# Attention of three layers in units of 256 rows, on row and column tiles of TensorE

## What is computed

```python
xn = _layernorm(x)
s = attention_k(xn)            # k = 0 to 3
g = _silu(ffn_k(xn))
x = x + s * g
```

```python
# layer 0: 16 query heads of 64, one head of keys and values, 2 null keys,
#          l2-normed q and k; the first 64 keys are open to every query
# layer 1: 16 heads of 64, each with its own keys and values
scores = einsum('bhsa,bhta->bhst', q, k) * scale
pattern = softmax(where(causal, scores, -1e5), axis=-1)
z = einsum('bhst,bhta->bsha', pattern, v); out = einsum('bsha,had->bsd', z, Wo) + bo
# layer 3: 16 heads of 8, no output product
```

## Time and profile before

| | us |
|---|---|
| median of three runs | 5998.41 |
| lowest run | 5994.97 |
| profiled execution, its span | 5995.4 |
| attention of layer 0, first scores to end of loops | 82 to 644 |
| the same, layer 1 | 1024 to 1573 |
| the same, layer 3 | 5158 to 5720 |

### The profile page before, as it was taken

The page is one execution under the profiler, slowest core; times in us unless marked ns, Lnnn a source line. Parts: engine busy times, 40 slices in busy tenths (PEclk is TensorE's granted clock), DMA queues, the critical chain, the costliest instruction groups (busy, mean ns, idle before and its releaser), DMA issues. The chain is left out here.

```text
span 5995.4 us, 91995 instructions
## 1 busy us (share of the span) xinstructions
PE 4804.1 (80%) x27408; PEld 3412.1 (57%) x27408; DVE 3795.6 (63%) x8398; ACT 3211.5 (54%) x9294; POOL 1986.0 (33%) x1579
## 2 busy tenths in 40 slices
PE   6888897999864446888888888888888887688888
PEld 4667664666631104566666666666666665466666
DVE  5555223444558886777777777777777776455522
ACT  4444343555323335666666766666766665244433
POOL 3333100222204553444444444444444442122200
PEclk8888998999975558999999999999999999688899
DMA  0000000000000001000000000000000000000000
GB/s 16 1 2 2 33 0 19 2 2 2 13 3 0 0 0 47 1 0 21 0 0 21 0 0 21 0 0 21 0 0 0 0 0 1 16 1 0 0 28 7
DMA packets 26030, 41.55 MB, mean 7 GB/s; under 512 B 12208, under 2 KB 18376, under 8 KB 25160
## 3 DMA queue, kind: packets, MB, share of 16 engines
q1 hardware_dynamic: 25800, 38.86, 1.9%
HBM read 36.75 MB, written 2.10 MB: 6 GB/s over the span
## 5 line engine op out<-in xcount | busy, mean ns | idle before, releaser
L1380 PE MATMUL ps<-l2f_wqkv,l2f_xsT 128*128 (+3 forms) x1536 | 741.6, 606 | 96.5 <-DVE xnT L1575 90.5
L1312 POOL TENSOR_TENSOR l2f_rn<-l2f_ss,neghalf 128x16 f32<-128x16 f32 x192 | 564.7, 2941 | 436.2 <-DVE l2f_ss L1569 436.2
L1757 ACT ACTIVATE l2f_p<-ps,l2f_negmax 128x96 f32<-128x96 f32 x1536 | 501.7, 339 | 281.8 <-DVE l2f_negmax L1600 278.2
L1318 POOL TENSOR_TENSOR l2f_cosd<-xnT,l2f_rot 128x1024 f32<-128x1024 f32 x192 | 487.0, 2541 | 174.8 <-DVE xnT L1575 174.8
L1438 PE MATMUL ps<-l2f_pT,l2f_vw 96*128 96x128 f32 x3072 | 419.7, 280 | 39.2 <-DVE l2f_pT L1622 38.9
L1380 PEld LDWEIGHTS ps<-l2f_wqkv,l2f_xsT 128*128 128x128 f32 (+1 forms) x1536 | 243.4, 178 | 347.4 <-issue 197.2
L1772 ACT COPY l2f_oT<-ps 64x256 f32<-64x256 f32 x768 | 281.3, 366 | 268.1 <-PE ps L1438 256.4
L1438 PEld LDWEIGHTS ps<-l2f_pT,l2f_vw 96*128 96x128 f32 x3072 | 379.4, 194 | 59.4 <-issue 54.2
L1338 POOL TENSOR_TENSOR l2f_rstd<-l2f_mv,neghalf 128x1 f32<-128x1 f32 x96 | 52.8, 550 | 1045.9 <-DVE l2f_mv L1634 1045.9
L1411 PEld LDWEIGHTS ps<-l2f_kT,l2f_qz 128*128 128x128 f32 x3072 | 398.3, 194 | 1.5 <-issue 0.4
L1411 PE MATMUL ps<-l2f_kT,l2f_qz 128*128 128x96 f32 x3072 | 397.9, 273 | 0.0
(11 more groups left out here) (348 smaller groups left out, 12274.8 us busy)
## 6 DMA issues: line engine op xcount, KB each, us to landing
l2f_wqkv<-L_ffn_Wqkv_dram SPq DMA_DIRECT2D x18, 512.0 KB
l0f_w<-L_w_dram SPq DMA_DIRECT2D x2, 2304.0 KB
l3f_w<-L_w_dram SPq DMA_DIRECT2D x2, 2048.0 KB
l2f_wo<-L_ffn_Wo_dram SPq DMA_DIRECT2D x6, 512.0 KB
l2f_w<-L_ffn_W_dram SPq DMA_DIRECT2D x6, 341.0 KB
l2f_b<-L_ffn_b_dram SPq DMA_DIRECT2D x6, 341.0 KB
l1f_w<-L_w_dram SPq DMA_DIRECT2D x1, 1152.0 KB
k_turn<-l3a_kF SPq DMA_DIRECT2D x4, 256.0 KB, 2.0
```

The source lines that it names most:

```text
L1312: nc.gpsimd.tensor_tensor(rn[:, k], ss[:, k], g.neghalf[:, 0:HEADS], ALU.pow).then_inc(rn_ready, 1)
L1318: nc.gpsimd.tensor_tensor(cosd[:, k].rearrange("p (h d) -> p h d", d=DH), nrm[:, k].rearrange("p (h d) -> p h d", d=DH), rot[:, k, 0, t].u ...
L1380: ins = nc.tensor.matmul(g.ps[0:rows, 2 * (k % 2) + hf], x, wqkv[:, bass.ds(weight_slot(it), 1), c0 + hf * 512:c0 + (hf + 1) * 512] .rearr ...
L1757: ins = nc.scalar.activation(p[:, n % 2, c], g.ps[:, 4, c * KW:(c + 1) * KW], ACT.Exp, bias=negmax[:, col:col + 1], accum_out=rowsum[:, co ...
```

## The change

The class `Softmax` becomes `PairSoftmax`. A unit n is now 256 rows, in two halves h of 128, and there are 32 units in a batch in each layer.

- Layer 0: a half is 8 heads by 16 queries. Layer 1: a half is one head by 128 queries. Layer 3: a half is 4 heads by 32 queries, and a block of 32 queries is two units. Keys go up in steps of 16, 128 and 32.
- Scores: each half contracts over its own rows only, 64 (32 in layer 3), with `lane(n, h)`. Queries need no zeros at other heads' rows in layers 0 and 1 (tile `qT`), and a quarter of `qz` in layer 3. The halves' products alternate, in pieces of 256 columns. The mask is added the same way, on the same rows; in layer 1 it is written first, by a product over the whole array.
- Outputs: each half multiplies with the values of its own head and writes to its own 64 (32) partitions of one bank, bank 7. Halves alternate by chunk.
- Transposes go to three banks in turn, and read full chunks, so `p` is cleared by GpSimdE in each batch of layers 0 and 3.
- One maximum and one reciprocal serve both halves; exp and the copies stay one per half. In layer 3 one copy is VectorE's and one ScalarE's; in layers 0 and 1 both are VectorE's. The output is collected in one copy.
- Orders: TensorE does scores of n+2, outputs of n-2, transposes of n. VectorE does copies of n-1, the reciprocal of n+1, the maximum of n+2, and in layer 3 the collection of n-3. ScalarE does exp of n+2, its copy of n in layer 3, the collection of n-2.

```diff
+    def pe_scores(self, pe, b, n):
+        pe.wait_ge(self.probs_ready, self.at(b, 0 if n < 2 else n if self.big(n) else n - 1))
+        pieces = self.pieces(n)
+        if self.mask_before is not None:
+            pieces = [(nk - P, nk)] + [(c0, min(c1, nk - P)) for c0, c1 in pieces if c0 < nk - P]
+            for h in range(2):
+                nc.tensor.matmul(s[:, h, nk - P:nk], self.g.identb[:], self.mask_before, start=True, stop=False)
...
+        for i, (c0, c1) in enumerate(pieces):
+            for h in range(2):
+                ins = nc.tensor.matmul(s[:, h, c0:c1], self.q(n, h), self.k(n, h, c0, c1),
+                                       start=self.mask_before is None or i > 0, stop=c1 <= m0 or self.mask_before is not None)
...
+    def pe_pv(self, pe, b, n):
+        pe.wait_ge(self.copied[0], self.at(b, n + 1))
+        pe.wait_ge(self.copied[1], self.at(b, n + 1))
+        pe.wait_ge(self.collected, self.at(b, n // self.every * self.every))
         chunks = self.chunks(n)
-        for c, c0, rows in chunks:
-            ins = self.nc.tensor.matmul(self.g.ps[:, 6 + n % 2, 0:P], self.v(n, c, rows),
-                                        self.pT[0:rows, n % 2, c * P:(c + 1) * P],
-                                        start=(c == 0), stop=(c == len(chunks) - 1))
+        for c in range(chunks):
+            for h in range(2):
+                ins = self.nc.tensor.matmul(self.g.ps[self.lane(n, h), self.PV_BANK, 0:P], self.v(n, h, c),
+                                            self.pT[:, n % 2, h, c * P:(c + 1) * P],
+                                            start=(c == 0), stop=(c == chunks - 1))
...
-        for n in range(self.steps):
+        for n in range(self.units):
             self.pe_scores(pe, b, n + 2)
+            self.pe_pv(pe, b, n - 2)
             self.pe_turn(pe, b, n)
-            self.pe_pv(pe, b, n - 1)
...
-        for n in range(self.steps + 1):
-            self.inverse_sum(dve, b, n + 1)
+        for n in range(self.units + 3):
+            if 1 <= n <= self.units:
+                for h in range(2):
+                    if self.copiers[h] == "dve":
+                        self.copy_turned(dve, self.nc.vector.tensor_copy, b, n - 1, h)
+            if n + 1 < self.units:
+                self.inverse_sum(dve, b, n + 1)
             self.maximum(dve, b, n + 2)
-            if n < self.steps and self.copier == "dve":
-                self.copy_turned(dve, self.nc.vector.tensor_copy, b, n)
-            if n >= 1 and self.copier == "act":
-                self.collect(dve, b, n - 1)
+            if n >= 3 and self.collector == "dve":
+                self.collect(dve, b, n - 3)
...
+            for h in range(2):
+                ins = self.nc.scalar.activation(self.p[:, n % 3, h, 0:nk], s[:, h], ACT.Exp,
+                                                bias=self.negmax[:, n, h:h + 1],
+                                                accum_out=self.rowsum[:, n, h:h + 1])
...
+PIECE = 256
...
-            nc.vector.memset(at.p[:], 0.0)
-            nc.vector.memset(qz[:], 0.0)
+            nc.vector.tensor_copy(spread[:], consts[:, 0:P])
+            nc.vector.tensor_copy(later[:], consts[:, P:P + QB])
...
+            sp.dma_start(consts[:, 0:P], g.c["spread16"]).then_inc(loaded, 16)
+            sp.dma_start(consts[:, P:P + QB], g.c["later16"]).then_inc(loaded, 16)
...
+                nc.gpsimd.memset(at.p[:], 0.0).then_inc(p_zeroed, 1)
...
-                        for hf in range(2):
-                            rows = slice(hf * DH, (hf + 1) * DH)
-                            ins = nc.scalar.activation(qz[rows, c, :, hf], g.ps[rows, i % 2].rearrange("p (i q) -> p i q", q=QB),
-                                                       ACT.Identity, bias=bq[rows, c:c + 1], scale=DH ** -0.5)
+                        ins = nc.scalar.activation(qT[:, c], g.ps[:, i % 2], ACT.Identity, bias=bq[:, c:c + 1],
+                                                   scale=DH ** -0.5)
...
-    QB = P // HEADS
-    GROUP = 8
+    LANES = 4
+    PER = HEADS // LANES
+    QB = P // PER
+    BLOCKS = SEQ // QB
+    GROUP = 4
```

More of the change, by code:

```diff
@@ L210, in pe_scores @@
     def pe_scores(self, pe, b, n):
-        if n >= self.steps:
+        if n >= self.units:
             return
-        nc, nk, mask = self.nc, self.keys(n), self.mask(n)
-        s = self.banks(n % 3)
-        pe.wait_ge(self.probs_ready, self.at(b, max(n - (1 if nk > 512 else 2), 0)))
-        for c0 in range(0, nk, 512):
-            c1 = min(c0 + 512, nk)
-            ins = nc.tensor.matmul(s[:, c0:c1], self.q(n), self.k(n, c0, c1), start=True, stop=mask is None)
-        if mask is not None:
-            m0 = nk - mask.shape[-1]
+        nc, nk = self.nc, self.keys(n)
@@ L466, in _ @@
                 ch.done(nc.vector.tensor_copy(kraw[:], kv[:, :, 0:DH]))
-                for half in range(2):
-                    ch.done(nc.vector.tensor_copy(v[:, :, half], kv[:, :, DH:2 * DH]))
+                ch.done(nc.vector.tensor_copy(v[:], kv[:, :, DH:2 * DH]))
                 ch.join()
```

290 lines of the change are left out of this document (171 added, 119 removed).

## The result

The changed kernel takes 5704.23 us (median of 4 runs, 5690.4 to 5734.64) against 5996.88 before: ratio 0.9519, 95% interval 0.9489 to 0.9549. It is faster, 293 us off where 235 were forecast. One of the four runs of the kernel before took 20161.61 us and is not in the ratio; the other three lie between 5994.97 and 5998.41. The profiled span is 5694.7 us.

The account below looks back on a forecast made before the run. TensorE, busy for 80% of the span, was taken to bound the kernel. Loops 150 us plus 85 around them, 235 off the profiled 5995.4, gave 5760, as a median 5765 (chance 0.52); range 5620 to 5990.

Parts of the forecast that it names:

- the staggered overlap, 2k+1 slots: TensorE's scores and outputs: halves overlap partly, 2k+1 slots instead of 4k; streams of 62, 70 and 60 us a batch.
- The case for no overlap: Rival: halves don't run side by side, streams 21, 19 and 21 us longer; 6026 us, chance 0.07.
- The change of division: TensorE switching between row halves, column halves and whole array: 0.17 us each, three a unit, four in layer 1.
- Nothing of the kind is in the trace.: Claim that the earlier kernel's trace shows no change of the array's division, so its price was bounded between 0 and 0.35.
- the rivals of free and of dear changes: Changes of the array's division cost nothing (5637 us, chance 0.15) or 0.35 us each (6009 us, chance 0.12).
- Seven per cent on top: Loops take 7% over TensorE's summed streams and changes, as in the earlier step (1.67 against 1.56 us).
- Slow clock at the start: Layer 0's loop: 20 us over the rule put down to the slow clock, so 16 added, giving 100.
- Layer 1's test: Layer 1's loop at full clock: 98 us right, 84 free changes, 120 or more dear changes or no overlap.
- the ring: Per unit two exps, one reciprocal, one maximum through ScalarE and VectorE: 67, 73 and 68 us a batch, under TensorE's.
- it is level, not longer: Path through collect, outputs, transposes, scores, maximum and exps: 5.5 us for two units, against 2 x 2.85 of TensorE.
- Slow clock as a rival: Idle half array keeps layers 0 and 3 at 1.2 GHz: 6053 us, 6309 with layer 1; chance 0.12.
- Around the loops: Savings outside the softmax loops, from masked queries, projection copies, clearings and merged copies: together 85 us.

Follow-up runs that it names:

- one_tile: Changed kernel with both halves' products on the first half's rows or columns of the array, outputs half after half; 6078.14 us, 1.0105 of the kernel before.
- outputs_one_behind: Changed kernel with TensorE's outputs of n-1 behind the transposes of n, and layer 3's collect ahead of reciprocal and maximum; 6082.84 us.
- collects_first: Changed kernel with unit n-3 collected ahead of the exp or maximum of n+2 in all layers; 5607.82 us.
- l3_collect_first: Changed kernel with VectorE's collect of unit n-3 in layer 3 moved ahead of the reciprocal and the maximum; 5605.97 us.

## Why the prediction was right, and where it wasn't

The time was forecast at 5765 and is 5704. The direction, the overlap and the price of a change held, but that the sum came so near is luck in part: by the forecast layers 0 and 1 gave 123 us too little, layer 3 gave 37 too much, and what lies around the loops 20 too much.

- *Streams.* The step that failed is the staggered overlap, 2k+1 slots. The halves run fully side by side: outputs every 0.055 us, and the scores of 402 keys in 0.73, where 5 of 8 slots would be 0.83. Over a batch of layer 0 that is 18 for transposes, 336 x 0.055 = 18.5 for outputs and about 15 for scores, 51 us where the forecast had 62. The case for no overlap, 6026, came near: one_tile is at 6078.
- *The change of division* was put at 0.17 and shows 0.17 at two of three places. The rule of the Trainium skill's "TensorEngine Tiling (Array Packing)", Key Properties, that changing the mode drains the engine, agrees with these idle times; it gives no size, and the size of one tail of a product was the right one. But layer 1 has no fourth change: its mask product uses the whole array and stands behind the transposes, which do too, with no gap (timeline of layer 1 below: the seventh transpose starts 0.27 before the end of its row, at 921.43, and the mask product 0.10 later).

```profile
920.77 0.93 PE L268 MATMUL ps<-ident,l1a_p 128*128 128x128 f32 x7
921.53 0.27 PE L236 MATMUL ps<-causal,identb 128*128 128x128 bf16 x2
```

- *"Nothing of the kind is in the trace."* It was. In layer 1 of the kernel before, every second step ends in a chunk of 64 keys, whose output product uses 64 rows among products that use 128:

```profile
1041.78 0.39 PE L246 MATMUL ps<-l1a_pT,l1a_v 128*128 128x128 f32 x2
1042.09 0.48 PE L246 MATMUL ps<-l1a_pT,l1a_v 64*128 64x128 f32 x2
1042.51 0.64 PE L219 MATMUL ps<-l1a_kT,l1a_qz 128*128 128x448 f32 x1
...
1043.76 0.61 PE L246 MATMUL ps<-l1a_pT,l1a_v 128*128 128x128 f32 x4
1044.20 0.59 PE L219 MATMUL ps<-l1a_kT,l1a_qz 128*128 128x512 f32 x1
```

  From the first of four output instructions to the next scores it is 0.73 us where the last two use 64 rows, and 0.44 where all use 128. That is 0.29 for going there and back, about 0.15 each. Read before the run, these rows could have priced the change, and taken weight from the rivals of free and of dear changes. They also mean that half of the steps of layer 1 paid two such changes already, about 9 us a batch.
- *The range of 5680 to 5870* for a change at 0.08 to 0.27 doesn't follow from the prediction's own terms: 10 changes a unit over the three layers, 32 units and 4 batches are 1280 changes, and 0.09 less or 0.10 more of each, with the 7%, gives 5640 to 5900.
- *Seven per cent on top.* Near enough. By the rule of 0.83 ns a column the round shown streams 0.64 for transposes, 0.67 for scores side by side and 0.64 for outputs, 1.95, and three changes add 0.51: 2.46, against 2.57 measured, 4 to 5% more.
- *Slow clock at the start.* The prediction put 20 us of layer 0's loop before down to it. The earlier trace rows don't bear that: 16 us at about half clock cost at most 8. In the kernel after, the loop takes 82.4, and 51 and 16 leave 15 of it, close to the 16 that was added, by luck: the half clock lasts for 22 us there, which costs at most 11, and TensorE is idle for 4.5.
- *Layer 1's test.* The prediction named 98 us as right and 84 as the mark of free changes. It is 84.8 with changes that cost about 0.17 each. That rival's sum for the ring (73 us and a seventh) fits in size, but its mechanism, free changes, is not what happened. A loop time alone couldn't tell the two, the idle time ahead of the weight loads could. TensorE is busy for 74 us of the 84.6 in a loop; what sets the loop is open.
- *Layer 3.* Forecast 104, in fact 113, though every stream is shorter than forecast. Two terms failed. One is "it is level, not longer": the path through collect and outputs was added up for a single unit, but VectorE collects two units at once into a single bank and behind the maximum, so every second unit waits, about 1 us in the mean and 16 a batch. The prediction had named this wait and priced it at nothing. The other is the 22 us for the slow clock, which took the stretch at half clock to be no longer than before; it is 61 to 102 us of a loop instead of 41 to 44. With the collect first both shrink together, and layer 3 takes 89, well under the forecast.
- *Slow clock as a rival.* Layers 0 and 1 nearly keep their clock (0.87 for 0.93 in the loop of layer 0, 1.00 in layer 1). In layer 3 this rival came true in part: its mean granted clock is 0.65 and 0.71 in the loops shown, against 0.83 before. That it didn't show in the total is because the overlap was fuller than forecast. And with TensorE waiting for ScalarE in every unit (outputs_one_behind) layer 1 fell to 0.70.
- *Around the loops.* 65 for 85. Layer 3's gaps gave 25 for 31; the query tiles are 0.62 each (0.56 forecast), the wait 3.27 (about 3). Layer 1's projection pairs take 1.90 us (rows below), for 1.75 forecast: 0.70 x 32 = 22 for 27, of which about 17 arrive (4.3 in each gap between batches). The clearings gave about 9 us ahead of layer 0 and 10 in layer 1 (ScalarE's wait of 22.01 in the earlier trace rows is 11.97 now), 19 for 16. Layer 0's merged copies gave 2.7 us over the three gaps where 2.7 a batch were forecast, 11: the half microsecond and more in each tile ahead of the last was hidden.

```profile
873.62 1.28 ACT L781 ACT_TABLE_LOAD   x1 [11.97 <-DVE l1a_bq L758]
...
880.82 0.69 ACT L781 ACTIVATE l1a_qT<-ps,l1a_bq 128x512 f32<-128x512 f32 x1 [0.36 <-PE ps L741]
...
882.73 0.69 ACT L781 ACTIVATE l1a_qT<-ps,l1a_bq 128x512 f32<-128x512 f32 x1 [0.36 <-PE ps L741]
```

## What to carry to other kernels

Two products that use different rows or columns of TensorE's array can run fully side by side, in f32 too. Here that is worth 374 us, and the changes of division cost about half of it (an estimate: 3 x 32 x 0.17 = 16 us a batch, 196 us over three layers of four batches); count the streams in halves, and 0.17 us for each change. When a pipeline gets fewer output banks, the instruction that empties the bank must stand ahead of anything that needs scores issued in the same round, or the outputs must stand a step later: its place on VectorE or ScalarE decided 98 us in one layer and 472 in two others, while the order on TensorE decided about 20. And before an instruction is said to be moved ahead, write two rounds of the queue out one after another: it may be the same circle, as with the copies of this change and the collects of collects_first. Look at the granted clock over every loop of a stage, since loops that do the same work stood at half clock for 61 to 102 us.

## What was not expected of the hardware

- Written order within a stage doesn't undo the overlap: two blocks of four score instructions, one per half, load in 0.74 us, the same as when they alternate (0.73); six and six outputs in 0.90 against 0.67 alternating and 1.28 on one tile.
- At the half clock the idle time ahead of each kind of product is 0.33 to 0.38 us, twice that of full clock (layer 3 of the kernel after):

```profile
5238.44 0.72 PEld L268 LDWEIGHTS ps<-ident,l3a_p 128*128 128x128 f32 x4 [0.38 <-issue]
...
5239.48 0.51 PEld L241 LDWEIGHTS ps<-l3a_kT,l3a_qz 32*128 32x128 f32 x4 [0.33 <-issue]
```

- In layer 3 TensorE was busy for 48.8 of 49.9 us by the profile and the clock was still 0.50. In that kernel the clock stayed at 1.00 through the loops only when products over the whole array were added ahead of them and in them. In one_tile TensorE was busy for 17.0 of 17.0 us of layer 1 at 0.50, where the kernel after, busy for 74 of 84.6 us, stood at 1.00 throughout the loop shown.

```profile
5136.10:5186.00 49.90, 48.83 (x284) 28.43 (x286) 22.81 (x68) 23.14 (x98) 14.34 (x20) 0.50 0.00 0
```

The row is of l3_collect_first. The Trainium skill, "TensorE: Matmul & The Clock Gate", Part 1, has the gate follow how busy TensorE is; by the busy time of the profile these two stretches speak against it, and what the gate counts can't be read from these rows.
